# Rotary step of a fused attention kernel: the rotated block is written to a buffer in SBUF instead of back into its PSUM bank

## The reference

```python
q = (c_q @ w_up_q.T).reshape(b, s, H, DH).transpose(0, 2, 1, 3)
k = (c_kv @ w_up_k.T).reshape(b, s, H, DH).transpose(0, 2, 1, 3)
# q and k, with e and o the even and the odd features of a head:
rot = jnp.stack([e * cos - o * sin, e * sin + o * cos], axis=-1)
attn = jax.nn.softmax(jnp.einsum('bhqd,bhkd->bhqk', q, k) / 8, axis=-1)
out = jnp.einsum('bhqk,bhkd->bhqd', attn, v)
```

## Time and profile before

| | |
|---|---|
| median of 3 runs | 3990.85 us (3990.67 to 3993.88) |
| profiled execution, its own time | 3990.85 us |
| its span from first to last instruction | 3989.1 us |
| PE busy | 3718.3 us, 93% |
| DVE busy | 2264.7 us, 57% |
| ACT busy | 1698.3 us, 43% |
| POOL busy | 2623.0 us, 66% |

### The profile page before, as it was taken

How to read it: one execution, slowest core, us unless ns; L and a number is a source line. 1 busy time by engine, 2 the same in 40 slices (tenths; PEclk the granted TensorE clock), 3 DMA queues, 4 the chain that set the end, 5 groups by cost and what they waited for, 6 DMA issues and landing times. The chain is left out here.

```text
span 3989.1 us, 59212 instructions
## 1 busy us (share of the span) xinstructions
PE 3718.3 (93%) x16736; PEld 2499.7 (63%) x16736; DVE 2264.7 (57%) x2984; ACT 1698.3 (43%) x3212; POOL 2623.0 (66%) x1471
## 2 busy tenths in 40 slices
PE   2899999999999999987874999999999999999799
PEld 2666666666666666646763566666666666666488
DVE  4444444444444444436654677777777777777344
ACT  1344444444444444434431444444444444444344
POOL 2577777777777777863213677777777777778511
PEclk9999999999999999998986999999999999999899
DMA  5444444344444444311014455555555455554100
GB/s 172 109 105 106 106 98 99 98 98 105 106 106 105 101 100 104 84 26 35 32 53 107 99 102 100 102 102 103 104 102 103 99 103 102 102 103 82 40 17 27
DMA packets 312425, 363.64 MB, mean 91 GB/s; under 512 B 144545, under 2 KB 182305, under 8 KB 308257
## 3 DMA queue, kind: packets, MB, share of 16 engines
q1 hardware_dynamic: 303808, 291.43, 35.0%
q10 hardware_dynamic: 8544, 71.31, 5.1%
HBM read 138.68 MB, written 21.50 MB: 40 GB/s over the span
## 5 line engine op out<-in xcount | busy, mean ns | idle before, releaser
L860 POOL TENSOR_TENSOR a_rs<-a_rs,a_p 128x1024 f32<-128x1024 f32 x384 | 914.6, 2382 | 287.8 <-ACT a_p L773 270.4
L787 DVE TENSOR_REDUCE a_nmax<-a_ps_x 128x1 fp32r<-128x1024 f32 x512 | 627.1, 1225 | 771.4 <-PE a_ps_x L605 771.4
L860 POOL TENSOR_TENSOR b_rs<-b_rs,b_p 128x1024 f32<-128x1024 f32 x384 | 915.8, 2385 | 219.1 <-ACT b_p L773 200.5
L787 DVE TENSOR_REDUCE b_nmax<-b_ps_x 128x1 fp32r<-128x1024 f32 x512 | 626.8, 1224 | 370.1 <-PE b_ps_x L605 332.5
L773 ACT ACTIVATE a_p<-a_ps_s 128x512 f32<-128x512 f32 x1024 | 528.9, 603 | 400.0 <-PE a_ps_s L619 375.3
L773 ACT ACTIVATE b_p<-b_ps_s 128x512 f32<-128x512 f32 x1024 | 529.2, 603 | 359.6 <-PE b_ps_s L619 337.7
L635 PE MATMUL a_ps_o<-a_p,a_v 128*64 128x512 f32 x2048 | 467.7, 598 | 0.0
L635 PE MATMUL b_ps_o<-b_p,b_v 128*64 128x512 f32 x2048 | 467.7, 598 | 0.0
L605 PE MATMUL b_ps_x<-b_k,b_q 128*128 128x512 f32 x1024 | 395.3, 468 | 35.2 <-DMA b_q<-b_nat_l 18.9
L618 PE MATMUL b_ps_s<-b_q,b_k 128*128 128x512 f32 x1024 | 415.6, 406 | 2.8 <-ACT b_p L773 1.6
L618 PE MATMUL a_ps_s<-a_q,a_k 128*128 128x512 f32 x1024 | 414.3, 405 | 1.1 <-DMA a_q<-a_nmax 1.1
(11 more groups left out here) (166 smaller groups left out, 5722.1 us busy)
## 6 DMA issues: line engine op xcount, KB each, us to landing
a_k<-a_nat_h SPq DMA_DIRECT2D x256, 128.0 KB, 2.4
a_q<-a_nat_h SPq DMA_DIRECT2D x256, 128.0 KB, 2.4
b_k<-b_nat_h SPq DMA_DIRECT2D x256, 128.0 KB, 3.8
b_q<-b_nat_h SPq DMA_DIRECT2D x256, 128.0 KB, 3.6
feat<-feat_a ACTq DMA_DIRECT2D x15, 2048.0 KB, 8.9
feat<-feat_b ACTq DMA_DIRECT2D x15, 2048.0 KB, 11.2
a_k<-a_nat_l SPq DMA_DIRECT2D x128, 128.0 KB, 2.4
a_q<-a_nat_l SPq DMA_DIRECT2D x128, 128.0 KB, 2.4
```

The source lines that it names most:

```text
L787: dve.reduce_max(nmax[:, g % 2, head, qi:qi + 1], ps_x[:].rearrange("p a b -> p (a b)"), AX_X, negate=True).then_inc(s_red, 1)
L860: pool.tensor_tensor(out, out, p[:, bb, i, :], ALU.add).then_inc(s_sum, 1)
```

## The change

Attention b gets a buffer `rot` of 128 x 512 in SBUF. The product with `cos_t` reads PSUM and writes `rot`; the addition of `turn` reads `rot` and writes `rot`; ACT and DVE make `nat_h` and `nat_l` from `rot`. PE may overwrite `ps_t[:, 0]` when the product with `cos_t` is done (the third of the four steps that `s_turn` counts per conversion), not when `nat_l` is. DVE's product with `cos_t` waits for the `nat_l` of the conversion before (its own earlier instruction, which frees `rot`) in place of the second product with `sin_t`. Attention a has no rotary step and keeps its operands. No instruction is added, removed or moved; operands and waits change.

```diff
-            turn = sb("turn", [P, BLOCK])
+            turn, rot = sb("turn", [P, BLOCK]), sb("rot", [P, BLOCK])
...
-            pe.wait_ge(s_nat_l, due(t, 8, n))
+            if rope is None:
+                pe.wait_ge(s_nat_l, due(t, 8, n))
+            else:
+                pe.wait_ge(s_turn, due(t, 32, 4 * n - 1))
...
-            act.activation(nat_h[:, half, :], ps_t[:, 0, :], ACT.Copy,
+            act.activation(nat_h[:, half, :], ps_t[:, 0, :] if rope is None else rot[:], ACT.Copy,
...
-            dve.wait_ge(s_turn, due(t, 32, 4 * n + 2))
-            dve.tensor_tensor(ps_t[:, 0, :], ps_t[:, 0, :], cos_t[:, cols], ALU.mult).then_inc(s_turn, 1)
+            dve.wait_ge(s_nat_l, due(t, 8, n))
+            dve.tensor_tensor(rot[:], ps_t[:, 0, :], cos_t[:, cols], ALU.mult).then_inc(s_turn, 1)
             dve.wait_ge(s_turn, due(t, 32, 4 * n + 3))
-            dve.tensor_tensor(ps_t[:, 0, :], ps_t[:, 0, :], turn[:], ALU.add).then_inc(s_turn, 1)
+            dve.tensor_tensor(rot[:], rot[:], turn[:], ALU.add).then_inc(s_turn, 1)
...
-            dve.scalar_tensor_tensor(nat_l[:, half, :], ps_t[:, 0, :],
+            dve.scalar_tensor_tensor(nat_l[:, half, :], ps_t[:, 0, :] if rope is None else rot[:],
```

## The result

The changed kernel takes 4093.53 us, the median of four runs (4089.03 to 4101.7), against 3991.88 us for the kernel before in the same session: 1.0256 times as long, with an interval of 1.0239 to 1.0274, or 101.6 us more. The forecast was 4103 us, 112 us more. Lines behind the change have new numbers: L790 is the reduce that was L787, L797 and L803 the products with sin and cos that were L794 and L800, L805 the sum that was L802, L810 the low part that was L807, L738 the high part that was L735, L684 the projection that was L681, L859 and L863 POOL's adds that were L856 and L860. The profiled execution took 4099.89 us, with a span of 4098.0 us; that is 109 us more than the profiled execution before, so differences between the two profiles add up to 109 us and not to 101.6.

A forecast was written before the change was run, and what follows sets the result against it. PE bounds attention b, busy 1425.6 of 1450 us. Blocking 91 plus clock 25 minus early release 4 gave +112 us on 3990.85, so 4103 us; range 4030 to 4180 us.

The forecast's parts named there:

- Blocking: In attention b, L802 and L807 with two SBUF inputs and POOL's SBUF-reading adds wait for each other's whole instruction: 91 us.
- two meetings in the feed-forward layer: L103 beside POOL's L443 took 2.29 us against 0.16 alone; L381 and POOL's L436 also slowed when they met.
- The walk: Eight attention b conversions (a body, repeating every 99 us) followed with both engines' shifts: 6.15 us a body, 91 us.
- the prediction without shifts: Those eight conversions laid over POOL's unshifted timeline: 12.0 us of waits, 7.3 us a body after margins, 108 us.
- The clock: In attention b, one PE stop over 2.4 us per body halves the clock for 3.3 us: 25 us in all.
- Early release: In the first projections PE no longer waits for `nat_l`: between 0 and 14.1 us won, about 4 us taken.
- The harsher one: Waiting DVE may lose to POOL's next add where POOL has no idle time, plus a second clock fall: 4188 us; 0.12.
- The milder one: In attention b, only the stop at conversion no. 1, which has no margin, is paid: 4030 us; chance 0.14.
- The faster one: In attention b, instructions of this length don't block each other and only the early release counts: 3982 us; chance 0.04.

## Why the prediction was right, step by step

The forecast of +112 us is near the 101.6 us measured, and the mechanism is the forecast one. The closeness of the number is in part luck: of its terms two were too large and one is missing, and they nearly cancel. In the profiles, where the stage grew by 107 us, PE's idle time rose by 69 us against 91 - 4 = 87 forecast, the clock took about 19 against 25, and 19 us more fall to the matmuls right behind the many stops, which no term of the sum held.

- **Blocking.** Forecast from two meetings in the feed-forward layer, both directions. Shown: the long durations at L805 and L810, their longest wait halved with POOL's add, and nearly all of them gone with it. The Trainium skill's rule (SBUF — State Buffer, "Who interferes with whom") holds in all of them: in every row above the later one waits until the other's instruction has ended, 123 of 123 at L805 and L810.
- **Waits and what is left of them.** The walk gave 6.15 us a body, 91 us in all; with the clock 7.6 us a body with the projections' gain taken off. Measured: a body of 106.5 in place of 99.4 us, 7.1 us. The sum was right within a tenth, its distribution less so. I had one stop of 2.95 us per body. PE's longest in the bodies are 1.67 us, two a body are near 1.57, and there are many short ones. DVE's waits are 9.4 us a body, where the prediction without shifts had 12.0. The walk let a blocked instruction run its whole 0.70 us behind POOL's end; it takes 0.55. It allowed POOL 11 us a body of its own waits; over the stage POOL is busy 40 us longer, 2.5 us a body.
- **A way that I left out.** I let all lateness reach PE by the reduce, and said that PE's wait for `b_nmax` would rise to around 100 us. It rose to 68.8, by 53. Another 27 us came by ACT, whose high part stands in front of the exponentials. The two together rose by 80 us, while other waits, those of the first projections and for DMAs and `b_o` among them, fell by 11.
- **The clock.** I took one fall per body, 25 us, for a stop of over 2.4 us. No such stop came in the bodies, but falls did. Between 2180 and 3700 us the granted clock is at 0.50 for 3.41 us twelve times, against twice before. One of them, by stretch, behind a stop of 1.57 us:

```profile
3339.40:3340.20 0.80, 0.00 (x0) 0.00 (x0) 0.76 (x1) 0.00 (x0) 0.64 (x1) 1.00 0.00 0
3340.90:3344.10 3.20, 3.20 (x9) 2.46 (x9) 1.22 (x1) 0.00 (x0) 3.12 (x2) 0.50 0.13 17
```

  That is 1.2 in place of 2.4 GHz after PE had been idle 1.57 us. Ten more falls at 1.7 us make 17 us, and PE's busy time at the low clock over the whole stage makes 19: a smaller term than forecast, behind shorter stops than I had thought would do it. This term was mis-sized and its reason was off; no run isolates it.
- **Early release.** Forecast 4 us. PE's waits in the first projections, 14.1 us for `nat_l` before, are 6.3 us for the product and 4.4 us for `v_next` now, 3.4 us less. What was late next was not DVE alone. ACT's third high part waits for a DMA to free `nat_h`, and its copies of the projected values stand behind it; before, then after:

```profile
2132.46 0.60 ACT L735 ACTIVATE b_nat_h<-b_ps_t 128x512 fp32r<-128x512 f32 x1 [7.68 <-DMA b_k<-b_nat_h]
```

```profile
2132.86 0.63 ACT L738 ACTIVATE b_nat_h<-b_rot 128x512 fp32r<-128x512 f32 x1 [7.76 <-DMA b_k<-b_nat_h]
```

  The time is nearly the same, though PE projects earlier. The DMA wait at the first maxima rose from 5.7 to 7.1 us. Little is left, and PE's old wait changes nothing that can be measured.
- **The rivals.** The harsher one, that POOL's next instruction gets in front of a waiting DVE where POOL has no pause, is out: L810 at 3376.22 ends 0.55 us after L863, and L859 with no pause between waited for it. The milder one had the right thought, the margins, but they swallowed most of the waits only where these were half as long. The faster one fell with the blocking.

## What to carry to other kernels

Before an operand is moved from PSUM to SBUF on VectorE, count the SBUF inputs that the instruction then has, and look whether GpSimd reads SBUF at that time; the place of the operand, not the duration of the instruction alone, sets the price. When such waits can't be avoided, a shorter GpSimd instruction makes the longest wait shorter, and a wait that fits in the slack of its consumer costs nothing: half the length took away 85% of the loss here. Count the stops as well as their length, since each one cost some 0.3 us beyond it. Follow an instruction that becomes late to all of its readers, the engine that has something else queued behind it included.

## What the runs showed of the hardware

- A blocked instruction ends a fixed time after its blocker: L810 at 3376.22 and L863's end at 3377.77 leave 0.55 us, which is less than the 0.69 us that the instruction takes alone. All 123 that waited leave 0.544 to 0.555 us. So some 0.14 us of it passes during the wait; 22 more started with at most 0.10 us of a POOL instruction left and took their 0.69 us.
- With one SBUF input there is no wait: in the kernel before, 161 of the 256 instructions of L802 and L807 started while a POOL instruction of over 1 us ran, and none took more than 0.70 us.
- In all 123 no further POOL instruction got in between, neither behind POOL's usual pause of 0.08 us nor, in 30 of them, where POOL shows no pause. The longest wait was 2.18 us.
- The granted clock fell to 0.50 behind stops of PE of 1.55 to 1.66 us, where the earlier trace rows had one of 2.40 us. Of the 30 stops of 1.5 to 1.7 us between 2180 and 3700 us, 11 had a fall behind them. The two falls of the kernel before stand behind stops of 1.44 and 1.12 us, so the length of the last stop alone does not tell.
